# A mixture-of-experts layer worked on its chosen token-expert pairs instead of on every pair

## The chip, the cores and the metric

The kernel runs on one core of a Trainium2 chip, in fp32. The time is device time in microseconds of one execution, from the device's own clock; the profile is of one further execution of the same program. PE is TensorE's matmuls, PEld its weight loads, DVE VectorE, ACT ScalarE, POOL GpSimd, SP SyncE, which issues most DMAs. A matmul of fp32 data stands in the records as two.

## What is computed

A small language-model tower of four layers on 2 x 1024 tokens with 128 features: embedding, attention and feed-forward parts of several kinds. Only its last part matters here, a feed-forward layer with 16 routed experts of which each token uses 2, and one shared expert that all tokens use:

```python
def _L3_ffn_ref(x, gate_w, gate_b, shared_w1, shared_b1, shared_w2, shared_b2, shared_act, expert_w1, ...):
    I, E, K = 96, 16, 2
    def swiglu5(h, alpha, gate_scale, up_shift, gate_clamp_raw, up_clamp_raw):
        gate_clamp, up_clamp = softplus(gate_clamp_raw), softplus(up_clamp_raw)
        g = clip(h[..., ::2], -gate_clamp, gate_clamp)
        u = clip(h[..., 1::2], -up_clamp, up_clamp)
        return g * sigmoid(g * alpha) * gate_scale * (u + up_shift)
    z = swiglu5(xf @ shared_w1 + shared_b1, *shared_act) @ shared_w2 + shared_b2
    w, idx = top_k(softmax(xf @ gate_w + gate_b), K);  w = w / sum(w)
    cw = sum(one_hot(idx, E) * w[..., None], axis=1)          # (tokens, E), two entries not 0
    he = einsum('nd,edh->enh', xf, expert_w1) + expert_b1
    oe = einsum('enh,ehd->end', swiglu5(he, ...), expert_w2) + expert_b2
    return einsum('ne,end->nd', cw, oe) + z
```

## The kernel before

Every part of the tower is a function of its own that opens blocks (one program for each engine, with a barrier of all engines at its end). Tokens are kept as 16 tiles of 128 (`m.h`, the residual, and `m.xn`, its normalised form, tokens on partitions; `m.xnT`, features on partitions).

The last layer is `stage_l3_ffn`. It issues six small loads on SP, then runs four pieces one behind the other: `layernorm`; `router` (logits of all tiles, twice a maximum over the experts, the two picks' softmax weights in `r.gates`, zero for the other 14 experts); `l3_expert_scalars` (the softplus of the clamps, biases turned so that the 96 hidden units lie on partitions); and `l3_experts`.

`l3_experts` works each of the 17 experts on all tokens, in 4 groups of 512, so 68 units. One unit n goes through five engines in turn: `up` on TensorE (two matmuls of 512 columns, gate and up half, L2252 and L2255), `fetch` on ACT (copies both out of PSUM with their bias, L2301 and L2304), `clip` on DVE (L2348, twice), `sigmoid` on ACT (L2310), `hidden` on POOL (two products, L2332 and L2334), `down` on TensorE (L2264, four matmuls of 128 tokens) and `add` on DVE (L2358, four times: the expert's weight for the token times the result, added to `m.h`). What a token's 14 other experts give is multiplied by zero there. Each engine's order is written out: TensorE does up of unit n+3 and then down of unit n, DVE clip of n+3 and add of n. The loop over experts is a hardware loop of two experts a turn.

SP loads an expert's weights (`load`: w1, 96 KB, L2226; w2, 48 KB, L2228) into one of two slots, as soon as the expert before last is done with it. The biases `b2` of all experts are added once, ahead of the loop, by a matmul of the gates (L2280).

## Time and profile before

| | us |
|---|---|
| median of 3 runs | 1853.22 |
| lowest and highest | 1851.44, 1855.21 |
| the profiled execution | 1853.36 |
| its span, first to last instruction | 1851.7 |
| start of `l3_experts` in the span | 1629.3 |
| issue of the output's store | 1846.2 |

Between those last two lies the part that is rewritten. The page's shares are over the whole span; what the last layer does is read from the groups, the timeline and the stretches of its own window. In a row, "[x <-E tile]" is idle time of that engine just before the row, and what ended it.

### The profile page before, as it was taken

How to read it: one execution, taken by the hardware profiler on the slowest of the kernel's cores; microseconds unless marked ns; L12 is line 12 of the kernel's file. 1: busy time of each engine (PE TensorE's matmuls, PEld its weight loads, DVE VectorE, ACT ScalarE, POOL GpSimd, SP SyncE). 2: the span in 40 equal slices, each digit the busy share in tenths (PEclk: the TensorE clock that was granted, in tenths of full speed). 3: DMA queues.
4: the chain of work that ended last, by engine and by line, in shares of the span. 5: the costliest groups of instructions: out<-in, count | busy, mean ns of one | idle time of the engine just before them, and what ended most of it. 6: DMA issues, size and time to landing. Idle time of an engine off the chain costs nothing. (4 is left out here: it accounts for less than half of the span.)

```text
span 1851.7 us, 29207 instructions
## 1 busy us (share of the span) xinstructions
PE 1548.6 (84%) x9758; PEld 1077.3 (58%) x9762; DVE 1229.8 (66%) x2401; ACT 851.2 (46%) x1058; POOL 731.1 (39%) x464
## 2 busy tenths in 40 slices
PE   2777999995899996134899999999999996579997
PEld 1545877794567774023456667666666664445554
DVE  5266345324211113974569999999999996669997
ACT  2243443431333432001456666666666673056664
POOL 2024423221000002631145555555555553249997
PEclk8888999997799998555899999999999998789998
DMA  3000000000100000000000000000000000000000
GB/s 105 1 1 1 2 1 1 1 2 1 30 17 17 17 12 1 0 0 1 1 1 1 1 0 0 0 0 0 0 0 0 0 0 1 2 13 13 13 13 27
DMA packets 22444, 13.68 MB, mean 7 GB/s; under 512 B 8075, under 2 KB 20774, under 8 KB 22118
## 3 DMA queue, kind: packets, MB, share of 16 engines
q1 hardware_dynamic: 21270, 12.20, 2.4%
q8 instruction: 46, 0.75, 0.2%
q10 hardware_dynamic: 1104, 0.53, 0.1%
q14 instruction: 24, 0.20, 0.0%
HBM read 11.67 MB, written 1.05 MB: 7 GB/s over the span
## 5 line engine op out<-in xcount | busy, mean ns | idle before, releaser
L1790 POOL TENSOR_TENSOR ta_ex<-ta_ex,ta_left 128x1024 f32<-128x1024 f32 x128 | 302.1, 2360 | 317.6 <-ACT ta_left L1743 316.9
L1702 PEld LDWEIGHTS ta_ps_o<-ta_exT,ta_vseq 128*32 128x32 f32 x2048 | 213.2, 110 | 101.9 <-ACT ta_exT L1735 88.2
L1653 PE MATMUL ta_ps_s<-ta_kT,ta_qz 128*128 (+1 forms) x512 | 242.6, 596 | 20.8 <-ACT ta_ex L1731 20.0
L1702 PE MATMUL ta_ps_o<-ta_exT,ta_vseq 128*32 128x128 f32 x2048 | 247.6, 274 | 6.4 <-ACT ta_exT L1735 6.4
L1735 ACT ACTIVATE ta_exT<-ta_ps_t 128x1024 f32<-128x1024 f32 x128 | 131.0, 1024 | 146.2 <-PE ta_ps_t L1682 146.2
L1808 DVE MAX8 ta_top<-ta_ps_s 128x8 f32<-128x1024 f32 x128 | 156.8, 1225 | 46.7 <-PE ta_ps_s L1653 46.7
L1232 DVE SCALAR_TENSOR_TENSOR h<-l1e_ps_d,l1f_gates,h 128x128 f32<-128x128 f32 x128 | 36.0, 344 | 191.7 <-PE l1e_ps_d L1171 191.7
L1815 DVE MATCH_REPLACE8 ta_left<-ta_top,ta_ps_s 128x1024 f32<-128x1024 f32 x128 | 155.3, 1214 | 0.0
L1820 DVE MAX8 ta_top<-ta_left 128x8 f32<-128x1024 f32 x128 | 154.7, 1209 | 0.0
L1825 DVE MATCH_REPLACE8 ta_left<-ta_top,ta_left 128x1024 f32<-128x1024 f32 x128 | 154.7, 1208 | 0.0
L1731 ACT ACTIVATE ta_ex<-ta_ps_s,ta_ntop 128x1024 f32<-128x1024 f32 x128 | 142.2, 1111 | 20.5 <-DVE ta_left L1815 19.8
L1212 ACT ACTIVATE l1e_hid<-l1e_ps_u,l1e_b 128x512 f32<-128x512 f32 x128 | 86.3, 688 | 141.8 <-PE l1e_ps_u L1160 111.8
L1743 ACT ACTIVATE ta_left<-ta_left,ta_ntop 128x1024 f32<-128x1024 f32 x128 | 147.0, 1148 | 1.4
L1682 PE MATMUL ta_ps_t<-consts,ta_ex 128*128 128x128 f32 x1024 | 137.9, 278 | 0.8 <-POOL ta_ex L1790 0.8
L1653 PEld LDWEIGHTS ta_ps_s<-ta_kT,ta_qz 128*128 128x128 f32 x512 | 87.3, 190 | 88.0 <-issue 74.4
L838 PEld LDWEIGHTS l1h_y<-l_v,l1h_score 128*128 128x128 f32 x1152 | 131.5, 192 | 11.6 <-issue 9.0
L838 PE MATMUL l1h_y<-l_v,l1h_score 128*128 128x65 f32 x1152 | 136.8, 277 | 1.6 <-issue 0.9
L1171 PEld LDWEIGHTS l1e_ps_d<-l1e_w,l1e_hid 128*128 128x128 f32 x1024 | 119.2, 192 | 14.9 <-issue 14.9
L1682 PEld LDWEIGHTS ta_ps_t<-consts,ta_ex 128*128 128x128 f32 x1024 | 111.9, 141 | 22.0 <-issue 18.6
L1160 PE MATMUL l1e_ps_u<-l1f_hT,l1e_w 128*128 128x512 f32 x256 | 118.5, 607 | 2.6 <-ACT l1e_hid L1212 2.6
L1171 PE MATMUL l1e_ps_d<-l1e_w,l1e_hid 128*128 128x128 f32 x1024 | 119.3, 275 | 0.0
L2332 POOL TENSOR_TENSOR l3e_sig<-l3e_gate,l3e_sig 96x512 f32<-96x512 f32 x68 | 98.7, 1451 | 39.0 <-ACT l3e_sig L2310 39.0
(526 smaller groups left out, 2478.8 us busy)
## 6 DMA issues: line engine op xcount, KB each, us to landing
l1e_w<-in_L_ffn_W_dram SPq DMA_DIRECT2D x16, 256.0 KB, 2.6
l3e_w<-in_L_ffn_expert_w_dram SPq DMA_DIRECT2D x16, 96.0 KB, 1.9
ids<-in_x_dram SPq DMA_DIRECT2D x1, 1024.0 KB
consts<-in_consts_dram SPq DMA_DIRECT2D x1, 1024.0 KB, 5.9
out_dram<-h SPq DMA_DIRECT2D x1, 1024.0 KB, 5.1
w_attn<-in_L_attn_w_attn_dram SPq DMA_DIRECT2D x1, 772.0 KB, 7.5
l3e_w<-in_L_ffn_expert_w_dram SPq DMA_DIRECT2D x16, 48.0 KB, 1.8
consts<-in_consts_dram SPq DMA_DIRECT2D x1, 394.5 KB
```

The source lines that it names most:

```text
L838: ins = pe.matmul(yps[:, head // 2, to:to + 65], score[:, job % RING, head, at:at + P], r.v[:, b * CH + j, 4 * quad + head, :], start=(kin ...
L1171: ins = pe.matmul(ps_d[:, u % 2, t * P:(t + 1) * P], hid[:, u % 2, c, t * P:(t + 1) * P], w2[:, k, c, :], start=(c == 0), stop=(c == 3))
L1653: ins = pe.matmul(ps_s[:, i % 2, half * BANK:(half + 1) * BANK], qz[:, odd, h, :], kT[:, grp, bass.ds(at.key0[i // PAIR] + half * BANK, BA ...
L1682: ins = pe.transpose(ps_t[:, j * P:(j + 1) * P], ex[:, i % 4, j * P:(j + 1) * P], m.ident)
L1702: ins = pe.matmul(ps_o[a:a + 2 * TW, grp * P:(grp + 1) * P], vseq[:, j, h, :], exT[:, i % 2, j, :], start=(j == 0), stop=(j == CH - 1))
L1731: act.activation(ex[:, i % 4, :], ps_s[:, i % 2, :], ACT.Exp, bias=ntop[:, i % 4:i % 4 + 1], scale=SC).then_inc(s_free, 1)
L1743: act.activation(left[:, i % 4, :], left[:, i % 4, :], ACT.Exp, bias=ntop[:, i % 4:i % 4 + 1], scale=SC).then_inc(left_exp, 1)
L1790: pool.tensor_tensor(ex[:, i % 4, :], ex[:, i % 4, :], left[:, i % 4, :], ALU.subtract).then_inc(kept, 1)
L1808: dve.max(top[:, i % 2, 0, :], ps_s[:, i % 2, :]).then_inc(max_done[0], 1)
L1815: dve.match_replace(left[:, i % 4, :], top[:, i % 2, 0, :], ps_s[:, i % 2, :], -BIG).then_inc(first_out, 1)
L1820: dve.max(top[:, i % 2, 1, :], left[:, i % 4, :]).then_inc(max_done[1], 1)
L1825: dve.match_replace(left[:, i % 4, :], top[:, i % 2, 1, :], left[:, i % 4, :], -BIG).then_inc(left_ready, 1)
```

## The change

The last layer computes only the two experts that a token chose.

- `router` also keeps its two picks as 0/1 tables (`r.picks`).
- A new function `slots` ranks the pairs. For each batch of 1024 tokens it gives every expert a run of whole blocks of 128 rows, long enough for its tokens, in expert order; 32 blocks a batch always suffice. It writes each pair's row number (`r.slot`), its weight (`r.share`) and each block's expert (`r.owner`).
- `stage_l3_ffn` clears two DRAM tensors of 4096 rows (2 MB each, `rows_dram`) with two DMAs from a tile of zeros. POOL's indirect stores put `m.xn` rows at their slots (`scatter`, 16 of 128 rows for each batch).
- `l3_expert_scalars` writes its biases, clamps and scale as a table in DRAM (`table_dram`, 17 x 96 x 8) and waits for it.
- `l3_experts` works 40 pairs of 128-row blocks, so 256 columns a pair: 8 pairs of the shared expert over all tokens, straight from `m.xnT`, then 32 pairs of routed blocks. A routed pair's rows are loaded (`rows`), transposed on TensorE (`turn`), copied by ACT (`flip`), and go through `up`, `clip`, `sigmoid`, `swish` (POOL, one product now), `hidden` (DVE, the other) and `down`; ACT copies the result (`keep`) and stores it to `outs_dram`.
- Each block may have another expert, so SP reads `r.owner` into a register for each block and loads w1, w2 and parameters at that address, into six slots.
- POOL gathers each token's two results back (`gather`, 16 a batch), and DVE adds them with their weights (`combine`) after the last pair. Batch 0's gathers run beside batch 1's pairs, batch 1's after the last store.
- Two constants are added (`before`, `firsts`, 160 columns, 80 KB). The loops over pairs are unrolled.

The diff's core:

```diff
@@ stage_l3_ffn
+                sp.wait_ge(zeroed, 1)
+                for b in range(B):
+                    sp.dma_start(r.rows_dram[b].rearrange("(n p) d -> p n d", p=P),
+                                 zero[:, :].unsqueeze(1).broadcast_to([P, L3_BLOCKS, D])).then_inc(r.s_cleared, 16)
...
         l3_expert_scalars(nc, m, r)
+        slots(nc, m, r, "l3k", L3_E, L3_BLOCKS, r.raw_act[:, 0:L3_E, 1])
         l3_experts(nc, m, r, w)
@@ l3_expert_scalars
+            sp.wait_ge(filled, 1)
+            sp.dma_start(r.table_dram.rearrange("e i k -> i e k"), table[:, :, :]).then_inc(r.s_table, 16)
+            sp.wait_ge(r.s_table, 16)
@@ l3_experts
+    E, G, NB = L3_E, L3_E + 1, L3_BLOCKS
+    SHARED, PAIRS = TILES // 2, TILES // 2 + B * NB // 2
+    STAGES = 6
...
         def _(sp):
...
+            def load(j):
+                for n in blocks(j):
+                    s, e = n % STAGES, sp.value_load(r.owner[0:1, n // NB, n % NB:n % NB + 1], min_val=0, max_val=E - 1)
+                    if n >= STAGES:
+                        sp.wait_ge(down_ready, SHARED + (n - STAGES) // 2 + 1)
+                    sp.dma_start(w1[:, s, :], w["L3_ffn_expert_w1"][bass.ds(e, 1), :, :].rearrange("e p f -> p (e f)")).then_inc(staged[s], 16)
+                    sp.dma_start(w2[:, s, :], w["L3_ffn_expert_w2"][bass.ds(e, 1), :, :].rearrange("e p f -> p (e f)")).then_inc(staged[s], 16)
+                    sp.dma_start(par[:, s, :], r.table_dram[bass.ds(e, 1), :, :].rearrange("e p f -> p (e f)")).then_inc(staged[s], 16)
...
+            for j in range(SHARED, PAIRS):
+                if j + 3 < PAIRS:
+                    rows(j + 3)
+                    load(j + 3)
...
+        def _(pool):
...
+            for j in range(SHARED):
+                if j < 4:
+                    for t, k in jobs[4 * j:4 * j + 4]:
+                        scatter(0, t, k)
+                swish(j)
+            for j in range(SHARED, SHARED + NB // 2):
+                swish(j)
+                for t, k in jobs[2 * (j - SHARED):2 * (j - SHARED) + 2]:
+                    scatter(1, t, k)
...
+            for k in range(4):
+                pool.wait_ge(y_out[k], 16 * 2 * NB // 8)
+            for t, k in jobs:
+                gather(1, t, k)
...
         def _(pe):
...
+            def up(j):
...
+                for k in range(2):
+                    if q >= 0:
+                        n = blocks(j)[k]
+                        pe.wait_ge(staged[n % STAGES], 48 * (n // STAGES + 1))
...
+            for j in range(PAIRS):
+                if j + 2 < PAIRS:
+                    up(j + 2)
+                down(j)
+                if SHARED <= j + 3 < PAIRS:
+                    turn(j + 3)
```

How this stands on SP and on TensorE. First SP in the hardware loop of before: one expert's w1 (L2226) and w2 (L2228), and the next expert's w1.

```order
L2226 ISA
L2226 DMA l3e_w1<-in_L3_ffn_expert_w1_dram 128x192
L2227 ISA
L2228 ISA
L2228 DMA l3e_w2<-in_L3_ffn_expert_w2_dram 96x128
```

Second, SP in the change, the loads of one routed block and the start of the next block's (L2276 is the register load of the block's expert, then w1, w2 and the parameters).

```order
L2276 TENSOR_LOAD l3f_owner
L2276 ISA x2
L2279 ISA
L2279 DMA l3e_w1<-in_L3_ffn_expert_w1_dram 128x192
L2280 ISA
L2280 DMA l3e_w2<-in_L3_ffn_expert_w2_dram 96x128
L2281 ISA
L2281 DMA l3e_par<-l3f_table 96x8
L2276 TENSOR_LOAD l3f_owner
```

Two DMAs for an expert, which served 2048 tokens, have become a register load and three DMAs for a block of 128 rows.

Third, TensorE in the loop of before: one unit's two up matmuls (L2252, L2255) and the four down matmuls (L2264) of the unit three before it.

```order
L2252 MATMUL l3e_ps_g<-xnT,l3e_w1 96x512
L2254 ISA
L2255 MATMUL l3e_ps_u<-xnT,l3e_w1 96x512
L2260 ISA
L2261 ISA
L2262 ISA
L2264 MATMUL l3e_ps_d<-l3e_w2,l3e_te 128x128 x4
```

Fourth, TensorE in the change, around the first routed pair's down: after up and down of the round before, turn of a pair (L2356), up of the same pair (L2373), down of the pair two before it (L2384; `w2_all` is the shared expert's).

```order
L2373 MATMUL l3e_ps_h<-l3e_xT,l3e_w1 96x128 x4
L2384 MATMUL l3e_ps_d<-l3e_w2_all,l3e_te 128x128 x2
L2356 MATMUL l3e_ps_x<-consts,l3e_x 128x128 x2
L2373 MATMUL l3e_ps_h<-l3e_xT,l3e_w1 96x128 x4
L2384 MATMUL l3e_ps_d<-l3e_w2,l3e_te 128x128 x2
```

Every matmul is of 128 columns now, eight a pair, and up of pair j+3 stands ahead of down of pair j+1, as it stood ahead of down before; but before, its weights changed only every fourth unit.

## Rows read from the trace of the kernel before

**Rows 1.** The page: each engine's busy us over the span
```profile
PE 1548.6 (84%) x9758; PEld 1077.3 (58%) x9762; DVE 1229.8 (66%) x2401; ACT 851.2 (46%) x1058; POOL 731.1 (39%) x464
```

**Rows 2.** The chain of waits, 1590 to 1852 us, shares by line
```profile
by line: POOL l3e_sig L2332 37.6%; issue 37.0%; POOL l3e_te L2334 5.2%; PE l3e_ps_d L2264 0.8%; POOLq L2331 0.8%; POOLq L2198 0.5%; DVE h L2358 0.3%; POOLq L2336 0.3%; POOLq L2333 0.1%; DVEq L2198 0.1%; DVEq L2355 0.0%; POOLq L2142 0.0%
```

**Rows 3.** Groups, 1560 to 1852 us: count, then busy us, mean ns, idle before
```profile
L2348 DVE TENSOR_SCALAR l3e_gate<-l3e_gate,l3f_limit 96x512 f32<-96x512 f32 x68 | 99.1, 1457 | 0.0
L2332 POOL TENSOR_TENSOR l3e_sig<-l3e_gate,l3e_sig 96x512 f32<-96x512 f32 x68 | 98.7, 1451 | 39.0 <-ACT l3e_sig L2310 39.0
...
L2358 DVE SCALAR_TENSOR_TENSOR h<-l3e_ps_d,l3f_gates,h 128x128 f32<-128x128 f32 x272 | 75.6, 334 | 4.0 <-PE l3e_ps_d L2264 4.0
...
L2348 DVE TENSOR_SCALAR l3e_up<-l3e_up,l3f_limit 96x512 f32<-96x512 f32 x68 | 37.3, 548 | 3.7 <-ACT l3e_up L2304 3.4
```

**Rows 4.** Timeline (start, duration, engine, line), expert loop, POOL
```profile
1720.59 1.46 POOL L2332 TENSOR_TENSOR l3e_sig<-l3e_gate,l3e_sig 96x512 f32<-96x512 f32 x1
...
1723.48 1.46 POOL L2332 TENSOR_TENSOR l3e_sig<-l3e_gate,l3e_sig 96x512 f32<-96x512 f32 x1
```

**Rows 5.** Timeline of SP's DMA issues, same columns
```profile
620.20 0.34 SPq L1135 DMA_DIRECT2D l1e_w<-in_L_ffn_W_dram  x1
620.74 0.37 SPq L1136 DMA_DIRECT2D l1e_b<-in_L_ffn_b_dram  x1
...
1595.80 0.35 SPq L2126 DMA_DIRECT2D l3f_gate_w<-in_L_ffn_gate_w_dram  x1
...
1629.88 0.42 SPq L2228 DMA_DIRECT2D l3e_w<-in_L_ffn_expert_w_dram  x1
1630.36 0.42 SPq L2235 DMA_DIRECT2D l3e_b<-in_L_ffn_expert_b_dram  x1
```

**Rows 6.** Timeline: second-matmul group, and the SP issue waiting for it
```profile
1656.52 1.15 PE L2264 MATMUL l3e_ps_d<-l3e_w,l3e_te 96*128 96x128 f32 x8
...
1657.86 0.32 SPq L2228 DMA_DIRECT2D l3e_w<-in_L_ffn_expert_w_dram  x1
```

**Rows 7.** DMA issues: count, size of each, median us from issue to landing
```profile
l3e_w<-in_L_ffn_expert_w_dram SPq DMA_DIRECT2D x16, 96.0 KB, 1.9
...
out_dram<-h SPq DMA_DIRECT2D x1, 1024.0 KB, 5.1
...
l1e_b<-in_L_ffn_b_dram SPq DMA_DIRECT2D x8, 2.0 KB, 2.3
```

**Rows 8.** Stretches: length, busy PE, PEld, DVE, ACT, POOL, then granted clock
```profile
865.00:870.00 5.00, 2.88 (x12) 2.07 (x12) 4.90 (x25) 1.17 (x2) 2.72 (x2) 0.50 0.00 0
1600.00:1620.00 20.00, 12.45 (x50) 10.30 (x50) 10.00 (x46) 2.39 (x4) 3.49 (x2) 0.50 0.00 0
1640.00:1842.00 202.00, 194.83 (x804) 101.77 (x802) 195.94 (x401) 133.00 (x202) 192.00 (x136) 0.98 0.04 11
```

**Rows 9.** Timeline: the last second matmuls and the output store
```profile
1842.58 2.08 PE L2264 MATMUL l3e_ps_d<-l3e_w,l3e_te 96*128 96x128 f32 x8 [0.48 <-POOL l3e_te L2334]
...
1846.17 0.41 SPq L2453 DMA_DIRECT2D out_dram<-h  x1
```

**Rows 10.** Timeline of the router and of the start of the expert block
```profile
1620.63 0.42 ACT L1060 ACTIVATE l3f_gates<-l3r_lg 128x256 f32<-128x256 f32 x1 [11.66 <-DVE l3r_lg L1088]
...
1623.58 0.42 DVE L1092 TENSOR_TENSOR l3r_kept<-l3r_kept,l3r_pick 128x256 f32<-128x256 f32 x1
1624.04 0.43 DVE L1094 TENSOR_TENSOR l3f_gates<-l3f_gates,l3r_kept 128x256 f32<-128x256 f32 x1
...
1629.32 1.28 ACT L2312 ACT_TABLE_LOAD   x1 [1.20 <-PEq L2142]
```

**Rows 11.** Groups of the whole span, two POOL forms
```profile
L1017 POOL TENSOR_TENSOR l1h_faded<-l1h_qk,l1h_fade 128x256 f32<-128x256 f32 x64 | 49.0, 800 | 41.0 <-ACT l1h_fade L964 35.8 <-DVE l1h_qk L868 5.2
...
L157 POOL TENSOR_TENSOR ln_l3f_small<-ln_l3f_small,neghalf 128x8 f32<-128x8 f32 x2 | 3.5, 1743 | 10.4 <-DVE ln_l3f_small L146 10.4
```

**Rows 12.** Instructions of line 2310: ns min/median/max, first and last start
```profile
L2310 ACTq FUSED_REGOPS  x64: 55/68/80, 1643.4 to 1826.0; - x64
```

More of the change, by code:

```diff
@@ new lines, in l3_experts, with blocks, weights @@
+        gates_turned, gates_in, bias_ready, bias_added, h_step = (
+            sem(k) for k in ("gates_turned", "gates_in", "bias_ready", "bias_added", "h_step"))
+        block = ctx.enter_context(nc.Block())
+        def blocks(j):
+            return [2 * (j - SHARED) + k for k in range(2)]
+        def weights(j, k):
+            if j < SHARED:
+                return w1_all[:, :], w2_all[:, :], par_all[:, :]
+            s = blocks(j)[k] % STAGES
+            return w1[:, s, :], w2[:, s, :], par[:, s, :]
@@ new lines, in up @@
+            def up(j):
+                q = j - SHARED
+                if j == 0:
+                    pe.wait_ge(shared_in, 48)
+                if q >= 0:
+                    pe.wait_ge(xT_ready, q + 1)
+                if j >= 2:
+                    pe.wait_ge(raised, j - 1)
+                for k in range(2):
+                    if q >= 0:
+                        n = blocks(j)[k]
+                        pe.wait_ge(staged[n % STAGES], 48 * (n // STAGES + 1))
+                    rows = r.hT[:, (2 * j + k) * P:(2 * j + k + 1) * P] if q < 0 else xT[:, q % 2, k * P:(k + 1) * P]
+                    for kind in range(2):
+                        ins = pe.matmul(ps_h[0:L3_I, j % 2, (2 * k + kind) * P:(2 * k + kind + 1) * P], weights(j, k)[0][:, kind::2], rows,
+                                        start=True, stop=True)
+                ins.then_inc(up_ready, 1)
@@ L2265, in down @@
+            def down(j):
+                pe.wait_ge(te_ready, j + 1)
+                if 2 <= j < SHARED + 2:
+                    pe.wait_ge(shared_added, j - 1)
+                elif j >= 2:
+                    pe.wait_ge(y_ready, j - 1 - SHARED)
+                for k in range(2):
+                    ins = pe.matmul(ps_d[:, j % 2, k * P:(k + 1) * P], te[:, j % 2, k, :], weights(j, k)[1], start=True, stop=True)
                 ins.then_inc(down_ready, 1)
-            for signal in (u_ready, down_ready):
-                pe.sem_inc(signal, FROM)
+            banks = [ps_x[0:G, 0, :], ps_x[0:G, 1, :], ps_d[0:G, 0, :], ps_d[0:G, 1, :]]
@@ new lines, in sigmoid, with keep @@
+            def sigmoid(j):
+                act.wait_ge(clipped, j + 1)
+                if j >= 2:
+                    act.wait_ge(t1_ready, j - 1)
+                    act.wait_ge(te_ready, j - 1)
+                for k in range(2):
+                    ins = act.activation(sig[:, j % 2, k, :], gate[:, j % 2, k, :], ACT.Sigmoid, scale=weights(j, k)[2][:, ALPHA:ALPHA + 1])
+                ins.then_inc(sig_ready, 1)
+            def keep(j):
+                q = j - SHARED
+                act.wait_ge(down_ready, j + 1)
+                if q >= 4:
+                    act.wait_ge(y_out[q % 4], 16 * (q // 4))
+                act.activation(y[:, q % 4, :, :], ps_d[:, j % 2, 0:2 * P].rearrange("p (k d) -> p k d", k=2), ACT.Copy).then_inc(y_ready, 1)
+                act.wait_ge(y_ready, q + 1)
+                b, n = q // (NB // 2), 2 * (q % (NB // 2))
+                act.dma_start(outs_dram[b][n * P:(n + 2) * P, :].rearrange("(k p) d -> p k d", k=2), y[:, q % 4, :, :]).then_inc(y_out[q % 4], 16)
@@ L2312, in _ @@
             act.activation(prime[:, :], m.pid, ACT.Sigmoid)
+            banks = [ps_x[0:G, 0, :], ps_x[0:G, 1, :], ps_d[0:G, 0, :], ps_d[0:G, 1, :]]
             for g in range(4):
                 act.wait_ge(gates_turned, g + 1)
[L2315 to L2320 removed]
@@ L2378, in _ @@
-            clip(LOOPS, 3)
-            for u in range(GROUPS):
-                add(LOOPS, u)
+            for j in range(PAIRS):
+                if j + 1 < PAIRS:
+                    clip(j + 1)
+                hidden(j)
+                if 1 <= j and j - 1 < SHARED:
+                    add(j - 1)
+            dve.wait_ge(shared_added, SHARED)
+            for b in range(B):
+                for t in range(CH):
+                    if t % 2 == 0:
+                        dve.wait_ge(gathered[b][t // 2], 64)
+                    combine(b, t)
```

372 lines of the change are left out of this document (230 added, 142 removed).

## The prediction

> **What bounds the kernel now.** I read the busy shares first [rows 1]: TensorE is the busiest engine over the whole span (84%), but that is a mean over all layers, and only the last one changes. So I took the chain of waits over that stage alone [rows 2]: its work is POOL's first product, 37.6%, and POOL's second product. The groups say why [rows 3]: 68 units (17 experts by 4 groups of 512 tokens), POOL's product 1451 ns in each, with 0 idle before it except the 39.0 us before the first unit. The timeline shows the pace [rows 4]: from one first product to the next but none between, 1720.59 to 1723.48, 2.89 us. 68 x 2.9 = 197 us, which is the length of the expert loop. The loop keeps TensorE busy 195 of 202 us at a granted clock of 0.98, the 2.4 GHz level [rows 8], so POOL is last by a few per cent and TensorE and DVE are right behind it. Nothing waits for a DMA there: a weight load is issued every 5 to 6 us and has a whole expert's time to land.
>
> **What the change takes away.** Of 17 x 2048 = 34,816 token columns, 8 x 256 + 32 x 256 = 10,240 are left. At the pace of rows 4 per 512 columns that would be 20 x 2.9 = 58 us in place of 197. That is the saving the new loop could have, if its 40 pairs went at 1.45 us. They don't, for the reason that follows.
>
> **The wait that takes its place.** In the second order excerpt (SP, the change) SP now has, for each block, a register load, then three DMAs; a pair has two blocks, so six DMAs. load(j+3) waits until down(j) is done (six staging slots are three pairs). TensorE in turn runs up(j+3) ahead of down(j+1). So nothing of down(j+1) can begin until weights that were only asked for after down(j) have landed. Queued behind that wait on SP are the whole load and the next rows(); behind the waiting up(j+3) on TensorE stand down(j+1) and the next turn; ACT's keep, and POOL and DVE one pair later, wait for those. This is a ring of length P, gone through once for every pair:
> - down(j) ends to first issue: 0.19 us (1656.52 + 1.15 = 1657.67 to 1657.86) [rows 6].
> - issue of DMAs at a register's address: 620.20 to 620.74, 0.54 us apart; at a fixed address 1629.88 to 1630.36, 0.48 [rows 5]. First block: two steps of 0.54 and 0.45 for the third itself, 1.53.
> - the second block's register load from SBUF, of which the trace of before has none: no less than a register operation on a queue, 0.07 us [rows 12], no more than a small DMA's round trip, 2.3 us [rows 7]. I take 0.5, nearer to the first, because no DMA queue and no completion signal are part of it; with 0.15 for the address arithmetic beside it.
> - second block: two more steps, 1.08, and the landing of the last, 1.9 us [rows 7] (3 KB of 32-byte rows, between the 1.9 of a 96 KB load and the 2.3 of a load of 4-byte pieces).
> - TensorE: 0.1 to wake, then four of the narrow matmuls, the second block's up and then down(j+1). Two of before's second matmuls take half of 2.08 us at the low clock [rows 9] for four, so two cost 1.04 at low and 0.58 at the high clock, where four take 1.15 [rows 6]. Together 2.08 or 1.16.
>
> Sum at the low clock 0.19 + 1.53 + 0.65 + 1.08 + 1.9 + 0.1 + 2.08 = 7.5 us; at the high clock 6.6. Which clock? TensorE has 8 matmuls in a ring, 4.2 us of 7.5 busy at the low clock. In the stretches of before where it was busy 58% and 62% of the time, the granted clock was 0.50, the 1.2 GHz level [rows 8]. I take 7.5. All else fits beneath it: DVE has 8 narrow instructions (about 0.3 us each, 334 ns the nearest [rows 3]), 2.4 us; ACT two copies of 256 columns and two of 128, at 0.42 for 256 [rows 10], plus one issue, 2 us; POOL a product of 256 columns, 0.80 [rows 11], and at most two indirect DMAs. SP itself: 6 x 0.54 + 2 x 0.65 + 0.48 = 5.0 us.
>
> The Trainium skill, in "DMA: Bandwidth & Descriptors", Latency and other measured facts, gives a floor of about 600 ns for such a load ("tensor_load"); no row here shows one. By it the ring would be 0.1 us longer and the time an estimated 3 us more.
>
> **The sum**, on the profiled execution (span 1851.7, its own time 1853.4, 1.7 more; the median of the runs is 1853.2):
> - The expert block starts at 1629.3 [rows 10]. Ahead of it now: two issues of the clearing DMAs, 0.9 [rows 5]; two copies of the picks, 0.5, on DVE whose pitch for 256 columns is 0.46 [rows 10]; the parameter table written to DRAM and waited for, 1632 rows of 32 bytes, between the 2.3 us of a small transfer and the 5.1 of the 2048-row store [rows 7], I take 4.0; and `slots`, 22 DVE instructions: ten of 256 columns at 0.46, three of 512 and two of 1024 at twice and some 2.5 times that, seven small ones at 0.15 to 0.2, 4.6 + 2.2 + 2.3 + 1.2 = 10.3 with a block change of 0.5. Together 16.2: the block starts at 1645.5. The clearing itself, 4 MB, is 4 x 5.1 = 20 us at most [rows 7], and is over by about 1620, hidden by layernorm and router.
> - From there to the end of the first routed pair: 16 scatters and four products on POOL, then the rows' landing and a round of the pairs. An indirect DMA's cost c on POOL is not in the trace: no less than an issue on SP, 0.4 [rows 5]; no more than 3.5, twice POOL's dearest small instruction of 1.74 us [rows 11]. I take 1.4, nearest to that instruction, since there too the time is POOL's own program and not data. 2 us start, 16 x 1.4, 4 x 0.8 make 27.6; landing of the last scatter and of the rows 2 x 2.3 make 32; then pairs 5 to 8 at about 4 each: 48 us. First routed down ends at 1693.5.
> - 29 rings (routed pairs 4 to 32 have their weights asked for this way): 29 x 7.5 = 217.5, to 1911. The last two pairs have nothing to wait for: 4.5, to 1915.5.
> - Tail: copy 0.5, store of the last pair landed 2.3; then 16 gathers on POOL, since all of batch 1 wait for that store, 16 x 1.4 = 22.4; landing 2.3; the last four additions 4 x 0.334 = 1.3 [rows 3]; the output store 5.5 to the end of the span [rows 9]. To 1949.8, with 1.7 **1951.5**, and 0.4 for 80 KB more constants at the kernel's start: **1952 us**, 5.3% slower.
>
> The result is the ring: break-even needs (1853.2 - 1952 + 217.5) / 29 = 4.1 us, and even with the lowest price of each of its parts (0.19, five pitches of 0.42, register 0.07, landing 1.9, TensorE 1.16) it is 5.4.
>
> **Rivals.**
> - *The ring at the cheap end*: TensorE holds the 2.4 GHz level (for: it holds 0.98 in the expert loop of before; against: there it is busy 96%). 29 x 6.6, and 4 less in front: 1952 - 26 - 4 = 1922. With the lowest parts, P = 5.4 and c = 0.6: 1952 - 61 - 4 - 22 = about 1865.
> - *POOL's indirect DMAs are dear*, c = 3: 16 x 1.6 = 25.6 more in front, as much in the tail, the ring itself untouched (0.8 + 2 x 3 = 6.8): 2003. For it: before's gate clip, 1457 ns against 548 for the same shape on `up` [rows 3], is DVE standing still while POOL runs, so the two do get into each other's way. The Trainium skill, in "SBUF — State Buffer", section "SBUF: two separate sides", says that descriptors of a DMA from POOL's queue are written through the port that a VectorE instruction in a two-port mode locks; by this rule c would grow with DVE's work, and this rival is where it would show.
> - *Faster than before*: the loads land in time, because the round of a pair through the engines (turn, copy, sigmoid, product, second product, down) is itself what sets the pace and SP runs ahead. At the high clock that round is 0.58 + 0.42 + 0.56 + 0.80 + 0.6 + 0.58 and 0.6 of signals, 4.1 us; with c = 0.7: 1952 - 29 x 3.4 - 4 - 11 - 11 = 1827. It decides from a ring under 4.1. For it: nothing in before waits for a DMA. Against it: there each load has an expert's whole time, and here the order of SP and TensorE makes the wait certain.
> - *The blocks don't shrink the work*: 32 blocks a batch are always worked, empty or not, so the number of rings is fixed at 29 whatever the routing; this moves nothing.
>
> **Chances.** The ring at about 7.5 with c near 1.4: 0.55. Cheap end (1865 to 1925): 0.22. Dear POOL, or a register load or landing so slow that the ring is 9 (1952 + 43): 0.16. Faster: 0.06, with 0.01 for no change. A difference under 0.2% is about what a measurement of this kernel cannot tell from none. The range of eight in ten: from 1885 (P = 6.0, c = 0.8: 1952 - 43.5 - 4 - 19) to 2015 (both of P = 8 and c = 2.8, or P = 9 and c = 2).
>
> **What would show it.** Right: TensorE's longest waits at up's matmuls, put down to the DMAs of the staged weights or parameters; down after down about 7.5 us apart over 29 pairs; SP's first issue of a pair 0.2 us after a down; granted clock 0.5 in the loop; POOL busy under half; some 20 us at the end in which POOL gathers and nothing else runs. Wrong: pairs under 4.5 us apart, or up waiting for xT and not for weights; the ring's step failed. POOL's queue full between the products: the third rival. A block start later than about 1650: the term of the table or of `slots` was too small.

## The result and the profile after

| | before | after |
|---|---|---|
| median, us | 1854.22 (4 runs) | 1948.32 (4 runs) |
| lowest and highest, us | 1851.44, 1855.69 | 1947.8, 1948.76 |
| span of the profiled execution | 1851.7 | 1947.1 |

The ratio is 1.0505, with a 95% interval of 1.0492 to 1.0518: 94 us slower, against a forecast of 1952 us. Line numbers of the new kernel are not those of before; L2373 is `up`, L2384 `down`, L2356 `turn`, L2320 POOL's product, L2279 to L2281 the three DMAs of a block and L2276 its register load.

The page's busy shares, to be read against [rows 1]:

```profile
PE 1489.1 (76%) x9494; PEld 1085.4 (56%) x9494; DVE 1154.1 (59%) x2386; ACT 762.4 (39%) x998; POOL 632.5 (32%) x437
```

Every engine does less than before (TensorE 60 us less, DVE 76, POOL 99), and the span is 95 us longer. So the time is in waits. These are the longest of the expert block (engine, line that waited, what it waited for: us in total, times, longest):

```profile
ACT l3e_xT L2418 <- PE l3e_ps_x L2356: 182.5, 32, 7.2
POOL l3e_sig L2320 <- ACT l3e_sig L2426: 176.2, 36, 6.8
DVE l3e_gate L2463 <- PE l3e_ps_h L2373: 111.9, 31, 5.6
PE l3e_ps_h L2373 <- DMA l3e_par<-l3f_table: 107.7, 58, 3.2
```

Read them upwards: ACT, POOL and DVE all wait for another engine, and that leads to TensorE; only TensorE waits for something outside, the third DMA of a block, 58 times, which is twice in each of 29 pairs. SP's own list has the other half of the ring: it waits for `down` as often as there are rings (the longest one is the first).

```profile
SPq L2279 <- PE l3e_ps_d L2384: 85.5, 29, 16.1
```

One ring in the timeline (start, duration, engine, line, operation; "[x <-E tile]" is idle time just before). Rows of other engines are left out:

```profile
1782.04 0.64 PE L2384 MATMUL l3e_ps_d<-l3e_w,l3e_te 96*128 96x128 f32 x2
...
1782.85 0.36 SPq L2279 DMA_DIRECT2D l3e_w<-in_L_ffn_expert_w_dram  x1
...
1783.38 0.33 SPq L2280 DMA_DIRECT2D l3e_w<-in_L_ffn_expert_w_dram  x1
...
1783.89 0.33 SPq L2281 DMA_DIRECT2D l3e_par<-l3f_table  x1
...
1784.98 0.36 SPq L2279 DMA_DIRECT2D l3e_w<-in_L_ffn_expert_w_dram  x1
...
1785.65 1.14 PE L2373 MATMUL l3e_ps_h<-l3e_xT,l3e_w 128*96 128x128 f32 x4 [2.56 <-DMA l3e_par<-l3f_table]
1786.02 0.32 SPq L2281 DMA_DIRECT2D l3e_par<-l3f_table  x1
...
1787.63 1.17 PE L2373 MATMUL l3e_ps_h<-l3e_xT,l3e_w 128*96 128x128 f32 x4 [0.84 <-DMA l3e_par<-l3f_table]
...
1788.60 1.06 PE L2384 MATMUL l3e_ps_d<-l3e_w,l3e_te 96*128 96x128 f32 x4
...
1789.83 0.36 SPq L2279 DMA_DIRECT2D l3e_w<-in_L_ffn_expert_w_dram  x1
```

`down` ends at 1782.68 (the first row shows the last two of its four records), SP issues 0.17 us later, the second block's parameters are issued at 1786.02, TensorE starts on them at 1787.63, and the next `down` ends at 1789.66: 6.98 us, of which TensorE works little and waits for DMAs twice. 29 such rings reach from 1696.7 to 1908.4, 211.7 us, 7.30 each; the one shown is among the shorter ones (they go from 6.91 to 8.41).

The stretches, to be read against [rows 8] (length, then busy PE, PEld, DVE, ACT, POOL with counts, granted clock, DMA share, GB/s): the loop, and the last gathers.

```profile
1697.00:1909.00 212.00, 103.74 (x405) 82.84 (x404) 71.33 (x234) 36.66 (x119) 49.36 (x57) 0.50 0.31 86
1916.00:1936.00 20.00, 0.00 (x0) 0.00 (x0) 5.89 (x17) 0.00 (x0) 15.12 (x17) 0.50 0.20 52
```

TensorE's granted clock was 0.98 in the loop of before and is 0.50, the 1.2 GHz level, in this one, where TensorE is busy 49%. POOL, which set the pace before, is busy 23%.

### The profile page after: what moved, and what is told of

It reads as the page before. It is cut to its first block and busy times, and to the rows that moved or that the text cites. A ratio compares the mean times of both kernels' runs of the same rounds, so it can differ in the third digit from the quotient of the medians.

```text
span 1947.1 us, 27871 instructions
## 1 busy us (share of the span) xinstructions
PE 1489.1 (76%) x9494; PEld 1085.4 (56%) x9494; DVE 1154.1 (59%) x2386; ACT 762.4 (39%) x998; POOL 632.5 (32%) x437
## 3 DMA queue, kind: packets, MB, share of 16 engines
q0 software_dynamic: 2048, 4.20, 0.7%
## 5 line engine op out<-in xcount | busy, mean ns | idle before, releaser
L1744 ACT ACTIVATE ta_exT<-ta_ps_t 128x1024 f32<-128x1024 f32 x128 | 131.0, 1024 | 145.6 <-PE ta_ps_t L1691 145.6
L2373 PE MATMUL l3e_ps_h<-l3e_xT,l3e_w 128*96 128x128 f32 x256 | 71.5, 435 | 109.1 <-DMA l3e_par<-l3f_table 107.7
L2373 PEld LDWEIGHTS l3e_ps_h<-l3e_xT,l3e_w 128*96 128x96 f32 x256 | 51.3, 264 | 130.8 <-issue 85.1
## 6 DMA issues: line engine op xcount, KB each, us to landing
l3f_rows<-l3f_zero SPq DMA_DIRECT2D x2, 2048.0 KB, 12.5
```

Source lines behind the costliest of these rows:

```text
L2373: ins = pe.matmul(ps_h[0:L3_I, j % 2, (2 * k + kind) * P:(2 * k + kind + 1) * P], weights(j, k)[0][:, kind::2], rows, start=True, stop=True)
```

## The experiments

Ten kernels, each timed beside the kernel before (1853.3 to 1853.8 us). Each differs from the changed kernel by what its diff shows.

### Is it the ring? Two ways to open it

**e1_swap**: on TensorE `down` goes ahead of the `up` that waits for the loads.

```diff
             for j in range(PAIRS):
+                down(j)
                 if j + 2 < PAIRS:
                     up(j + 2)
-                down(j)
```

> One edit: in TensorE's loop down(j) stands ahead of up(j+2) instead of behind it; same matmuls, same DMAs. Theory (the ring: the loads of pair j+3 wait for down(j), and down(j+1) stands behind up(j+3)): the ring now spans two pairs, since down(j+1) no longer stands behind the waiting up(j+3). Load chain 0.2 + 3.2 + 1.6, up 1.1, then clip, product and down of pair j+2, 4 us: some 9.5 us for two pairs, so 4.7 to 5.0 us a pair in place of the 7.3 of the changed kernel, as much as SP itself needs for its issues (4.7). 29 x 2.4 = 70 us less: 1865 to 1895 us. Rival A (the pairs' own way through the engines at the low clock sets the pace): nothing changes, 1940 to 1955. Rival B (the DMA system can't deliver more than a pair's 290 KB of weights in 7 us): the waits move, the pace stays, 1940 to 1955.

Measured: 1918.64 us, ratio 1.0349 (1.0331 to 1.0366). The waits for loads are gone, 30 us came back, and that is little more than half of the least that I had expected (53). What TensorE waits for now:

```profile
PE l3e_ps_d L2384 <- DVE l3e_te L2478: 62.2, 25, 3.1
```

One round in its timeline, rows between left out:

```profile
1754.44 0.71 PE L2384 MATMUL l3e_ps_d<-l3e_w,l3e_te 96*128 96x128 f32 x4 [2.57 <-DVE l3e_te L2478]
...
1754.99 1.68 PE L2373 MATMUL l3e_ps_h<-l3e_xT,l3e_w 128*96 128x128 f32 x8
...
1756.47 0.63 PE L2356 MATMUL l3e_ps_x<-consts,l3e_x 128*128 128x128 f32 x2
...
1757.14 0.38 ACT L2418 ACTIVATE l3e_xT<-l3e_ps_x 128x256 f32<-128x256 f32 x1 [4.00 <-PE l3e_ps_x L2356]
...
1757.42 0.68 ACT L2426 ACTIVATE l3e_sig<-l3e_gate,l3e_par 96x128 f32<-96x128 f32 x2
...
1758.18 0.80 POOL L2320 TENSOR_TENSOR l3e_sig<-l3e_gate,l3e_sig 96x256 f32<-96x256 f32 x1 [4.43 <-ACT l3e_sig L2426]
...
1759.01 0.61 DVE L2478 SCALAR_TENSOR_TENSOR l3e_te<-l3e_up,l3e_par,l3e_sig 96x128 f32<-96x128 f32 x2
1759.68 1.22 PE L2384 MATMUL l3e_ps_d<-l3e_w,l3e_te 96*128 96x128 f32 x4 [2.57 <-DVE l3e_te L2478]
```

Behind the first ring stood a second: `down`, `up`, `turn`, and then ACT, whose sigmoid stands behind the copy of the turned rows, POOL, DVE and `down` again, 1754.44 to 1759.68 = 5.24 us (mostly 5.3 to 5.9 over the loop). `up`, now no longer late, still stands in front of `turn`. So the ring through the DMAs is shown as the cause of the 7.3 us, and my expectation was wrong in leaving the other engines' own order out.

A third ring of almost the same length goes through DVE's order: `clip` of pair j+2 stands ahead of `hidden` of pair j+1, so `down`, `up`, `clip`, `hidden`, `down` is closed too. In the round shown `clip` ends at 1759.06 and POOL's product at 1758.98, so which of the two holds a routed pair can't be told apart. The first shared pairs have no turned rows beside them, POOL's product is over 3 us before `hidden`, and there DVE's order alone holds the pace, at 5.4 us a pair; the eight shared pairs of the changed kernel are 2.3 to 6.6 apart. That is where a part of the expected gain went: the 29 rings took 165.2 us instead of 211.7, 46 less, but the first routed `down` ends at 1710.3 instead of 1696.7, 14 us later, and the last two pairs take 2.6 us more.

**e2_eight**: eight staging slots, the loads four pairs ahead, so a load is asked for one pair earlier than `up` needs it.

```diff
-    STAGES = 6
+    STAGES = 8
...
-            for j in range(SHARED, SHARED + 3):
+            for j in range(SHARED, SHARED + 4):
                 load(j)
...
                 if j + 3 < PAIRS:
                     rows(j + 3)
-                    load(j + 3)
+                if j + 4 < PAIRS:
+                    load(j + 4)
```

> Order on TensorE as in the change, but eight staging slots and loads four pairs ahead. Theory: a load has a full pair's time more, so the ring is open and the pace falls to what SP needs for a pair's issues, 4.7 to 5.1 us: 1870 to 1895 us, with the waits at up mostly gone or short. Rival A (pairs' way through the engines): 1940 to 1955. Rival B (DMA rate): 1940 to 1955, landings longer than 1.6 us.

Measured: 1892.55 us, ratio 1.0211 (1.0194 to 1.0228), as expected. The same 29 pairs are 5.4 us apart on average. SP's waits for `down` fell, most of what is left being the first:

```profile
SPq L2279 <- PE l3e_ps_d L2385: 25.4, 16, 16.3
```

`up` waits for no DMA any more. What TensorE waits for now, beside ACT's copy, is the load of the rows (window 1697 to 1851), which SP issues behind a pair's six weight DMAs:

```profile
PE l3e_ps_x L2357 <- DMA l3e_x<-l3f_rows: 28.2, 27, 2.1
```

SP itself waits for only 9.2 us in these 154, so its queue is nearly always at work; why the pairs are 5.4 apart and not 4.7 is in part this load that comes late, in part issues that took longer (four of 0.9 to 1.6 us). In e10_deep below, which asks for the rows earlier too, that wait is no longer among the large ones.

### How large are the parts of the ring?

**e3_nopar** leaves out the third DMA: routed blocks use the shared expert's biases, clamps and scale, so that part of the computation is not the reference's.

```diff
-                    sp.dma_start(par[:, s, :], r.table_dram[bass.ds(e, 1), :, :].rearrange("e p f -> p (e f)")).then_inc(staged[s], 16)
...
-            return w1[:, s, :], w2[:, s, :], par[:, s, :]
+            return w1[:, s, :], w2[:, s, :], par_all[:, :]
```

> The third DMA of each block, its 3 KB of parameters, is left out; routed blocks use the shared expert's biases, clamps and scale, so part of the computation is another one at the same cost. Six slots, old order. Theory: the ring is shorter by two of SP's steps of 0.52 us, less some 0.2 for a w2 load landing later than a parameter load: 0.85 us, 29 times, 25 us less: 1918 to 1930. Rival A: no change. Rival B (DMA rate): 3 KB of 147 KB is 2%, 4 us less at most.

Measured: 1938.00 us, ratio 1.0457 (1.0425 to 1.0488). 10 us instead of 25, and the four executions lie far apart (1931.5 to 1942.2, the profiled one at 1934.0). What TensorE waits for:

```profile
PE l3e_ps_h L2372 <- DMA l3e_w<-in_L_ffn_expert_w_dram: 95.1, 57, 3.0
```

The issues left out do shorten SP's part by two steps, but the last DMA of a block is now one of 48 KB. In a ring of 6.8 us `up` begins 2.13 us after its issue, where it began 1.61 us after that of the parameters in the ring shown above. Over all 29 rings of both profiles, SP's part is 1.06 us shorter, as expected, but `up` of the second block begins 2.50 us after the last issue instead of 1.86, so a w2 load costs 0.64 us more than a parameter load, where I had put 0.2. The rings took 199.3 us instead of 211.7. Rings of over 8 us occur as well: in one, `up` begins 4.3 us after the last issue.

**e5_fill** puts nine matmuls of the identity on a free PSUM bank into every pair on TensorE, where it would wait.

```diff
+            def fill(count):
+                for _ in range(count):
+                    pe.matmul(ps_b[:, 0, 0:P], m.ident, m.one, start=True, stop=True)
...
+                if q >= 3:
+                    fill(6)
                 for k in range(2):
+                    if q >= 3 and k == 1:
+                        fill(3)
```

> Nine matmuls of the identity onto a free PSUM bank are added to each of 29 pairs, six ahead of up and three between its two blocks, where TensorE stands still for the loads; nothing reads them. Theory: TensorE's own part of the ring (2.03 us at the low clock) is 1.15 if the granted clock then stays at the 2.4 GHz level: 29 x 0.88 = 25 us less, 1920 to 1930, granted clock over 0.9 in the loop. If the clock stays at 0.5 the fillers take 0.42 x 2 each and partly stand behind the landing: up to 1 us a pair more, 1950 to 1980. Rival (the clock is part of no limit): no change although the clock rises.

Measured: 1932.63 us, ratio 1.0430 (1.0413 to 1.0448). More work made the kernel 15.7 us faster. Its stretches in the loop:

```profile
1700.00:1760.00 60.00, 42.47 (x281) 36.98 (x281) 22.06 (x72) 11.07 (x36) 18.98 (x21) 0.90 0.34 95
1760.00:1820.00 60.00, 42.79 (x307) 36.65 (x305) 23.00 (x75) 11.35 (x38) 7.85 (x10) 0.97 0.34 90
1828.00:1905.00 77.00, 49.48 (x294) 43.97 (x294) 29.39 (x96) 13.22 (x42) 28.17 (x31) 0.77 0.32 86
```

With TensorE busy 71% the granted clock is 0.90 and 0.97 in place of 0.50, and most rings are 6.1 to 6.6 us; in the last stretch the clock is 0.77. On average a ring is 0.52 us shorter than in the changed kernel (6.78 against 7.30). TensorE's part, from `up` of the second block to the end of `down`, is 1.13 us in most rings in place of 2.02, the 0.88 expected; but in seven of the 29 it is 1.9 to 2.0, as at the low level, which leaves 0.70 on average. And SP's part is 0.26 us longer on average (3.50 against 3.24), through late issues: in the longest ring, 9.04 us, one took 1.62 us instead of 0.33.

Such late issues and landings occur in all four kernels with the ring of six slots and three or two DMAs a block; a closed ring passes each of them on in full. The traces show what goes with them. Beside the kernel's own DMAs they have transfers on two queues whose kind the profile names "instruction", of 16 and of 8 KB. Of the 116 rings of the changed kernel, e3_nopar, e5_fill and e4_clear (below), 14 are over 8 us (2, 2, 4 and 6), and in each of the 14 such a transfer starts; of the 70 rings without one the longest is 7.47 us. The fillers are instructions too, and with them there are more transfers of 16 KB in the window 1640 to 1910 (packets, MB, share; first row the changed kernel, second e5_fill):

```profile
q8 instruction: 5, 0.08, 0.1%
q8 instruction: 9, 0.15, 0.2%
```

No run takes these transfers away, so this is what stands beside the late DMAs, not a shown cause.

**e4_clear** moves the two clearing DMAs from the stage's start into the router's block.

```diff
@@ stage_l3_ffn
-                sp.wait_ge(zeroed, 1)
-                for b in range(B):
-                    sp.dma_start(r.rows_dram[b]..., zero...).then_inc(r.s_cleared, 16)
@@ router
+            @block.sync
+            def _(sp):
+                sp.wait_ge(r.s_zeroed, 1)
+                for b in range(B):
+                    sp.dma_start(r.rows_dram[b]..., zero...).then_inc(r.s_cleared, 16)
```

> Only the two clearing DMAs are moved: from the stage's first block, whose end all engines wait for, to the router's block, where SP has nothing else. Theory: in the changed kernel's trace their two issues held SP for 5.84 us, not the 0.9 that was forecast, and layernorm started that much later; here they are issued beside the router's matmuls and landed long before the first scatter. 5.5 us less than the changed kernel: 1942 to 1944 us. Rival (the 5.84 us are hidden behind something else that is late, or the DMAs' traffic slows the scatters instead): 1947 to 1950.

Measured: 1945.52 us, ratio 1.0485 (1.0468 to 1.0503), 2.8 us less; the two intervals of ratio, this one and the changed kernel's, just overlap. The stage's first load and the expert block's are 6.0 us nearer to each other than in the changed kernel (1599.00 to 1645.52, against 1597.48 to 1649.98), so the issues' 5.9 us now lie beside the router. In the profile the 29 rings gave 5 us of that back: they took 217 us instead of 212, with six over 8 us instead of two. Clearing costs the same to issue there (5.87 us); it only stands where no engine waits for SP.

**e9_pack6** copies w1 and w2 of all experts into one DRAM tensor while the kernel's first layers run, with the parameters behind them, so that a block takes one DMA of 164 KB instead of three. Slots and lookahead stay.

```diff
+        m.pack = nc.dram_tensor("l3_pack", (L3_E + 1, P, 2 * L3_I + D + 8), F32).ap()
...
-                    sp.dma_start(w1[:, s, :], ...).then_inc(staged[s], 16)
-                    sp.dma_start(w2[:, s, :], ...).then_inc(staged[s], 16)
-                    sp.dma_start(par[:, s, :], ...).then_inc(staged[s], 16)
+                    sp.dma_start(ws[:, s, :], m.pack[bass.ds(e, 1), :, :].rearrange("e p f -> p (e f)")).then_inc(staged[s], 16)
```

> The change with one edit: an expert's w1, w2 and parameters lie packed in one DRAM tensor, so a block takes one DMA of 164 KB in place of three; the slots stay six, the loads three pairs ahead, so the closed ring stays. It separates the two edits that the packed and deeper run had made together. My theory, by the measured parts of a ring: 0.18 to the first issue, 1.09 to the second block's one issue (register load, address, issue), a landing of 2.3 instead of 1.6 us since the DMA carries 164 KB and not a small piece, and 2.03 of TensorE at the low clock, together 5.6 in place of 7.3; 29 x 1.7 = 49 off 1948: about 1899 (1893 to 1910). Rival: the depth alone was what counted, and a packed load lands so much later that the ring stays near 7: about 1940.

Measured: 1908.41 us, ratio 1.0292 (1.0274 to 1.0309), within what I expected, near its upper end. The 29 rings took 166.3 us, 45.4 less than in the changed kernel, where the whole kernel is 39.9 us faster: the packing is not free. Its DMAs stand in SP's queue at the kernel's start, and in the profile the last layer's first load comes 5.4 us later (1602.85 against 1597.48; in the unpacked kernels it lies between 1595.2 and 1599.0). The DMA issues (size, median us to landing) and one ring:

```profile
l3e_ws<-l_pack SPq DMA_DIRECT2D x64, 164.0 KB, 2.3
```

```profile
1748.09 1.42 SPq L2278 DMA_DIRECT2D l3e_ws<-l_pack  x2
...
1750.54 2.20 PE L2370 MATMUL l3e_ps_h<-l3e_xT,l3e_ws 128*96 128x128 f32 x8 [2.20 <-DMA l3e_ws<-l_pack]
1752.54 1.06 PE L2381 MATMUL l3e_ps_d<-l3e_ws,l3e_te 96*128 96x128 f32 x4
...
1753.77 0.33 SPq L2278 DMA_DIRECT2D l3e_ws<-l_pack  x1
```

From issue to issue 5.68 us, where the parts gave 5.6. The ring is still closed, TensorE still waits for a DMA in every pair, and its length is again the sum of its parts; over all 29 they are 0.17, 1.11, 2.44 and 2.01, together 5.73. This is the best test of the prediction's way of adding up, since here the sum was written before the run, from measured parts.

### What is the limit when the ring is open?

**e10_deep**: depth alone, 12 staging slots, six slots for rows, loads and rows five pairs ahead.

```diff
-    STAGES = 6
+    STAGES = 12
...
-        x, xT = sb("x", [P, 4, 2, D])...
+        x, xT = sb("x", [P, 6, 2, D])...
...
-                if j + 3 < PAIRS:
-                    rows(j + 3)
-                    load(j + 3)
+                if j + 5 < PAIRS:
+                    rows(j + 5)
+                if j + 5 < PAIRS:
+                    load(j + 5)
```

> The change with depth alone: 12 staging slots, loads and rows five pairs ahead, six row slots, three DMAs for a block, the order on TensorE and ACT as in the change. It separates the depth from the order in the run that had both (1868.8). My theory: the first six pairs run from loads made early, at about 3 us, and the rest go at SP's own 4.9 us a pair, as in that run, because the order decides nothing while SP sets the pace: 1866 to 1876. Rival: the order gave a part of its own, since a pair's round through the engines shows where loads are early: 1880 or more, near the 1892.6 of eight slots.

Measured: 1866.04 us, ratio 1.0070 (1.0053 to 1.0087). 82 of the 94 us are back with depth alone. After a start with prefetched loads, in which pairs are 3.4 to 4.1 us apart, SP sets the pace with 4.7 us a pair, at times 5 to 7.6, and waits for nothing:

```profile
1760.56 0.36 SPq L2279 DMA_DIRECT2D l3e_w<-in_L_ffn_expert_w_dram  x1
...
1765.28 0.36 SPq L2279 DMA_DIRECT2D l3e_w<-in_L_ffn_expert_w_dram  x1
```

The DMAs are those of the changed kernel, so a limit of the DMA engines at 7.3 us a pair is ruled out.

**e6_order**: the same depth, and also `turn` ahead of `up` and `down` on TensorE and the sigmoid ahead of the copy on ACT (the second ring of e1_swap taken apart).

```diff
             for j in range(PAIRS):
+                if SHARED <= j + 3 < PAIRS:
+                    turn(j + 3)
                 if j + 2 < PAIRS:
                     up(j + 2)
                 down(j)
-                if SHARED <= j + 3 < PAIRS:
-                    turn(j + 3)
...
+                sigmoid(j)
                 if SHARED <= j + 2 < PAIRS:
                     flip(j + 2)
-                sigmoid(j)
```

> Twelve staging slots with loads five pairs ahead, six row slots with rows five pairs ahead, TensorE's turn ahead of up and down, ACT's sigmoid ahead of its flip. The same DMAs. Theory: neither the loads nor the way turn, flip, sigmoid, product, down closes a ring now, so the pace is SP's own: 4.9 us a pair by the eight-slot kernel's trace. 31 x 4.9 = 152 us in place of its 160.5: 1880 to 1888 us, SP without waits. Rival (the DMA system at 110 to 120 GB/s is near what it gives these sizes): landings grow and the pace stays at 5.3, 1890 to 1895.

Measured: 1868.77 us, ratio 1.0080 (1.0063 to 1.0097), better than I had expected, but no better than e10_deep: while SP sets the pace, the order of the others decides nothing. I had underrated the depth and not known which edit carried it; e10_deep settles that.

**e7_pack**: the packed tensor of e9_pack6 with the depth of e10_deep, old order.

```diff
-    STAGES = 6
+    STAGES = 12
...
+                    sp.dma_start(ws[:, s, :], m.pack[bass.ds(e, 1), :, :].rearrange("e p f -> p (e f)")).then_inc(staged[s], 16)
```

> All experts' w1, w2 and parameters are first copied in DRAM into one tensor of 128 rows an expert (at the kernel's start, on SP's queue), so a block needs one DMA instead of three; same depth as the previous kernel, but the change's old order on TensorE and ACT. Theory: SP needs 2.9 us a pair, so the pace is the way of a pair through the engines: turn 0.7, flip 0.4, sigmoid 0.7, product 0.75, second product 0.6, down 1.2 and signals, 4.4 us at the low clock, 3.6 if TensorE's denser work brings the 2.4 GHz level back. 31 x 4.4 = 136: about 1868 us (1840 to 1875). Rival (DMA rate, 168 KB a block): pace 5 or more, 1885 or more.

Measured: 1846.44 us, ratio 0.9947 (0.9927 to 0.9966), the first that is faster than before. Pairs are 4.14 us apart at first, at a granted clock of 0.50 (1699 to 1720), and then 3.43 at 1.00 for most of the loop, with hardly a variation: no DMA and no SP in it, but the second ring, through turn, copy, sigmoid, product and `down`:

```profile
PE l3e_ps_d L2382 <- DVE l3e_te L2476: 25.5, 25, 3.5
```

**e8_all**: e7_pack with the order of e6_order and the clearing of e4_clear.

```diff
-    STAGES = 6
+    STAGES = 12
...
+                if SHARED <= j + 3 < PAIRS:
+                    turn(j + 3)
                 if j + 2 < PAIRS:
                     up(j + 2)
                 down(j)
-                if SHARED <= j + 3 < PAIRS:
-                    turn(j + 3)
...
+                sigmoid(j)
                 if SHARED <= j + 2 < PAIRS:
                     flip(j + 2)
-                sigmoid(j)
```

> The packed weights, the depth, the new order and the moved clearing together. Theory: nothing but the engines' own work is left. TensorE's eight matmuls at the low clock are 4.2 us a pair, at the high clock 2.3; at the high clock DVE's 2.6 and, while it scatters, POOL's 3.2 set the pace. With the high clock 31 x 3.1 = 96 us in place of 160.5 of the eight-slot kernel, and 5.5 less for the clearing: about 1822 us, faster than the kernel before (1812 to 1845). If the clock stays at 0.5: 31 x 4.3 = 133, 1860. Rival (DMA rate): 1880 or more.

Measured: **1817.00 us**, ratio 0.9793 (0.9776 to 0.9809), 37 us faster than before and 131 faster than the change as it was made. Where the order was worth nothing under SP's pace, it is worth 0.9 us a pair here. A stretch of its loop, and two `down` in it:

```profile
1700.00:1740.00 40.00, 25.59 (x199) 22.43 (x197) 37.24 (x114) 18.80 (x56) 22.57 (x27) 1.00 0.84 228
```

```profile
1725.50 0.71 PE L2387 MATMUL l3e_ps_d<-l3e_ws,l3e_te 96*128 96x128 f32 x4 [0.73 <-DVE l3e_te L2481]
1728.04 0.71 PE L2387 MATMUL l3e_ps_d<-l3e_ws,l3e_te 96*128 96x128 f32 x4 [0.73 <-DVE l3e_te L2481]
```

2.54 us a pair at the 2.4 GHz level; DVE is busy 37.24 of 40 us, by that share the bound now, with the DMA engines at 0.84 close behind. No run tests that.

## Why the prediction was right, step by step

**The mechanism.** That the ring through `down`, SP, the DMAs and `up` replaces POOL's pace was right: it is seen in the waits, and it opens in e1_swap, e2_eight and e10_deep, which leave the work as it is. Its length was forecast at 7.5 and is 7.30:

| part of the ring | forecast | in the ring shown | mean of 29 |
|---|---|---|---|
| `down` to first issue | 0.19 | 0.17 | 0.18 |
| first block's issues | 1.53 | about 1.5 | |
| register load and address | 0.65 | about 0.6 | |
| second block's two steps | 1.08 | 1.04 | |
| these three together | 3.26 | 3.17 | 3.24 |
| last issue to TensorE's start | 1.9 + 0.1 | 1.61 | 1.86 |
| `up` of a block and `down`, low clock | 2.08 | 2.03 | 2.02 |
| sum | 7.5 | 6.98 | 7.30 |

The means are taken from all issues and matmuls of the loop. No term is off by more than 0.14 us, so here the sum is right because its parts are. The ring shown is shorter than the mean because its last landing is: in the 11 rings in which POOL neither scatters nor gathers (1747 to 1826) TensorE starts 1.68 us after the last issue on average, and in the 11 behind them, in which it gathers batch 0, 2.08, the longest being 3.04 in the ring of 8.41. By the profile's own figure the parameters land 1.5 us after their issue at least, 1.6 in the median and 3.0 at most. The forecast had no row for that spread; its 2.0 lay within it. 29 rings of 0.2 us less make 6 us less than forecast. The register load's own price, for which before had no row, with the two steps beside it (ns, least/median/most):

```profile
L2276 SPq TENSOR_LOAD <-l3f_owner x55: 263/268/284, 1700.9 to 1898.0; - x55
L2276 SPq FUSED_REGOPS  x55: 152/152/155, 1701.2 to 1898.3; - x55
L2276 SPq SEQ_ASSERT  x55: 18/18/18, 1701.4 to 1898.5; - x55
```

The three are 0.44 us. From the issue before to the first after, 1783.89 to 1784.98, it is 1.09, of which 0.51 is the issue's own step, so the term put at 0.65 measured 0.58. The floor of about 600 ns of the Trainium skill ("DMA: Bandwidth & Descriptors", Latency and other measured facts) is not seen: 268 ns in the median of these rows.

**The clock.** The choice of the low level was right (0.50), and e5_fill shows what it costs: TensorE's part of a ring is 1.13 us in most of its rings against 2.02 here, where the forecast had 1.16 and 2.08. The shortest rings are 6.09 and 6.91.

**The block's start** was forecast for 1645.5 and came at 1649.98, 4.5 us late: here lay the term that was wrong by most, 0.9 us forecast and 5.84 measured. The rows (SP):

```profile
1599.87 5.84 SPq L2150 DMA_DIRECT2D l3f_rows<-l3f_zero  x2
...
1635.49 0.35 SPq L2189 DMA_DIRECT2D l3f_table<-l3s_table  x1
...
1649.98 0.35 SPq L2292 DMA_DIRECT2D l3e_w_all<-in_L_ffn_shared_w_dram  x1
```

Two issues of the clearing were priced at 0.9 us by the pitch of small DMAs [rows 5]; they hold SP for 5.84, and the block ends only with them: layernorm's first DVE instruction is at 1606.15. Hiding the data (two DMAs of 2 MB, 12.5 us to landing) was right and the issue was not. With the copies of the picks the part up to the table grew by 4.7 us, where 1.4 was forecast; e4_clear, which only moves the two issues, makes that part shorter again by 6 us. Table and wait took 3.05 us, 2.6 net of the block change that was there before, forecast 4.0; `slots` and its block change 11.4, forecast 10.8 (by its own unit prices the forecast should have added 2.8 and not 2.2 for the three instructions of 512 columns, and would have come to 11.4). The stage itself began 1.7 us later than in the profile of before (1597.48 against the 1595.80 of [rows 5]), which is within what one profile differs from the next: the unpacked kernels, whose earlier layers are the same, begin it between 1595.2 and 1599.0.

**POOL's indirect DMAs** had the widest bounds, 0.4 to 3.5, and I took 1.4. The scatters:

```profile
L2309 POOL DMA_INDIRECT l3f_rows<-xn,l3f_slot x32: 954/958/1244, 1650.8 to 1744.1; - x32
...
DMA to landing us min/median/max: 2.2/2.4/3.3
```

0.96 us and 0.30 us before the next, so c = 1.25, for gathers too. The front, from the block's start to the first routed `down`, came to 46.7 us against 48. The rule of the Trainium skill ("SBUF — State Buffer", "SBUF: two separate sides") by which such DMAs would grow with DVE's work, and which stood behind the rival of dear indirect DMAs, shows no effect here: median 958 ns for the scatters, which ran beside DVE's work, and 946 for the gathers. Which of DVE's instructions ran in a two-port mode no row shows, so this is no test of the rule itself.

**The tail** was forecast at 34.3 us after the last `down` and took 34.2 (1912.91 to 1947.1), by errors that cancel, which is luck. The gathers' last and the last additions:

```profile
1935.08 0.94 POOL L2313 DMA_INDIRECT l3e_back<-l3e_outs,l3f_slot  x1 [0.30 <-issue]
```

```profile
1937.71 1.51 DVE L2491 SCALAR_TENSOR_TENSOR h<-l3e_back,l3f_share,h 128x128 f32<-128x128 f32 x4 [3.53 <-DMA l3e_back<-l3e_outs,l3f_slot]
1941.57 0.41 SPq L2667 DMA_DIRECT2D out_dram<-h  x1
```

16 gathers took 20.0 us instead of 22.4 (1916.36 to 1936.3) and began 3.45 us after the last `down` instead of 2.8, as POOL was still at batch 0's; the last one's landing held the additions up by only 1.4 us more, where 2.3 was added; and between the last addition (1939.22) and the output's store lie 2.35 us, of which the forecast had nothing. The trace shows what ends them, the end of POOL's program in the block (ns, start):

```profile
L2230 POOLq DRAIN  x1: 18441/18441/18441, 1922.9 to 1922.9; - x1
```

It ends at 1941.33, 5.30 us after POOL's last gather instruction (1936.03), while DVE's own is over at 1939.52; the barrier and the store (1941.57) follow within 0.24 us. In the profiles of e1_swap, e4_clear, e5_fill, e7_pack, e8_all, e9_pack6 and e10_deep the same 5.3 us lie between them. What POOL does in them isn't shown.

**The rivals.** The faster one, in which the engines' own round sets the pace, was the next bound in fact: e7_pack shows that round. It was priced at 4.1 us for the high clock and is 3.43 there; the 4.14 that e7_pack shows at first are at the low one, and that they agree with the price is luck. It took another kernel, with the loads early, to reach it. In the cheap rival, 32 indirect DMAs at 0.6 instead of 1.4 us are 25.6 us less and not 22, so it ends at 1861 and not 1865. The break-even of 4.1 us a ring fits as well: e10_deep with 4.4 us on average is 0.7% slower than before, e7_pack with 3.4 to 4.1 is 0.5% faster.

**The total.** 1948.3 against 1952 looks better than the parts are: on the profiled execution the block's start is 4.5 us late, the front 1.3 short, the rings 5.8 short and the tail 0.1 short. The mechanism was right; that the total is off by only 0.2% is in part luck.

**What stays open.** Why single landings and issues take up to 1.9 us more while instruction transfers run, whether those are the cause, and why landings are longer while POOL gathers; and what POOL does in the 5.3 us at the block's end. For none of these was an experiment made.

## What to carry to other kernels

Before slots are counted, write down where each queue waits: if a load is asked for when the work of pair j ends, and the consumer's queue puts the load's user ahead of pair j+1, then the load's whole latency is in every round; slots help only as far as they let the load be asked for earlier, and here one pair more than the consumer's lookahead opened the ring (7.30 to 5.4 us). A changed order of one engine can close another ring elsewhere, as the shared pairs of e1_swap show, so look at the parts that were fast before as well. When a unit of work shrinks (here from an expert's 2048 tokens to 128 rows), count the DMA issues and register loads per unit, since they don't shrink with it; at half a microsecond each they are the next bound, and packing what is loaded together into one DMA removes it, at the price of making the packed copy (here 5 to 7 us at the kernel's start). Then look for the ring behind the ring: an order that changes nothing under one bound (e6_order against e10_deep) was worth 0.9 us a pair under the next.

## What the hardware did that was not expected

- A DMA's issue can cost far more than 0.5 us of the queue: the clearing DMAs of 2 MB each, 4096 rows of 512 B, held SP for 2.9 us each (5.84 for the two), while loads of 96 KB took 0.36. It was this issue that delayed the other engines, since all wait for the block's end; for the data, 12.5 us to landing, nothing waited.
- A load of a register from SBUF on SP took 0.27 us, where a parameter DMA takes 1.6 us to land.
- Matmuls without use made the kernel 15.7 us faster (1948.32 to 1932.63), as the granted clock of the loop rose from 0.50 to 0.90 and 0.97 in its first two stretches and 0.77 in the last.
- All 14 rings of over 8 us, in four kernels, have a transfer of an "instruction" queue in them.
- The store of the output was issued 2.35 us after the last addition; before it was 0.28 (the addition's end at 1845.89, the store at 1846.17). POOL's last instruction in the block ended 5.3 us after its last gather, in every kernel looked at.
